# Cross-attention on Trainium2: values projected from tiles of 128 context rows across four batches, then sorted by key

## What is computed

```python
Q = (query @ Wq.T + bq).reshape(B, Sq, 16, 16).transpose(0, 2, 1, 3)
K = (key_value @ Wk.T + bk).reshape(B, Skv, 16, 16).transpose(0, 2, 1, 3)
V = (key_value @ Wv.T + bv).reshape(B, Skv, 16, 16).transpose(0, 2, 1, 3)
attn = softmax(einsum('bhqd,bhkd->bhqk', Q, K) / 4)
context = einsum('bhqk,bhkd->bhqd', attn, V).transpose(0, 2, 1, 3).reshape(B, Sq, 256)
y = context @ W_o.T + b_o + query
out = (y - mean(y)) / sqrt(var(y) + 1e-5) * ln_gamma + ln_beta
```

## Time and profile before

| | us |
|---|---|
| median of three runs | 213.75 (213.46 to 214.18) |
| the profiled execution | 215.56 |
| its span, first to last instruction | 213.5 |
| PE, DVE, ACT, POOL busy | 192.7, 175.5, 173.4, 152.6 |
| mean granted clock of TensorE | 0.98 of full speed |

### The profile page before, as it was taken

One profiled execution on the slowest core, in us unless ns is written; L12 is line 12 of the kernel. 1 busy time (PEld: TensorE's weight loads), 2 busy tenths in 40 slices (PEclk: granted clock), 3 DMA queues, 4 the chain that ended last, 5 costly groups with the idle time before them and its releaser, 6 DMA issues.

```text
span 213.5 us, 5610 instructions
## 1 busy us (share of the span) xinstructions
PE 192.7 (90%) x2070; PEld 173.8 (81%) x2070; DVE 175.5 (82%) x391; ACT 173.4 (81%) x313; POOL 152.6 (71%) x148
## 2 busy tenths in 40 slices
PE   7898999979999989989998999999999999896830
PEld 4897999869899978977988798879788979795730
DVE  5879985657797898989898989898988997982694
ACT  4588789979888979998999899989998998889130
POOL 9976542596557766896689678867887788979653
PEclk9999999999999999999999999999999999999695
DMA  5945521403656964795479438943793188111112
GB/s 183 350 101 138 146 51 40 163 28 95 204 108 176 240 205 97 186 242 159 86 195 249 136 83 206 244 136 80 187 250 71 53 217 236 54 49 54 49 49 98
DMA packets 32978, 30.39 MB, mean 142 GB/s; under 512 B 11306, under 2 KB 27672, under 8 KB 32952
## 3 DMA queue, kind: packets, MB, share of 16 engines
q1 hardware_dynamic: 31720, 28.78, 51.3%
q10 hardware_dynamic: 1232, 1.26, 2.0%
HBM read 11.32 MB, written 4.19 MB: 73 GB/s over the span
## 4 chain that ended last, share of the span: by engine, by line
PE 29%; POOL 28%; issue 16%; SPq 10%; ACT 6%; DMA 5%; DVE 4%; POOLq 0%; ACTq 0%; DVEq 0%
POOL p_l L1150 18%; PE ps_x L417 14%; PE ps_acc L417 6%; PE ps_s L417 6%; POOL result L1158 5%; SPq L341 4%; POOL rs_y L1171 3%; ACT p_h L786 3%; PE ps_d L417 3%; SPq L302 3%; DMA q_mix<-q_high 3%; DMA w_raw<-in_wkT 2%; DVE result L1016 2%; SPq L319 1%; DVE xT_l L861 1%
## 5 line engine op out<-in xcount | busy, mean ns | idle before, releaser
L1150 POOL TENSOR_TENSOR p_l<-p,p_h 128x512 f16<-128x512 f32 x80 | 95.2, 1195 | 43.2 <-ACT p_h L786 42.3
L967 DVE TENSOR_REDUCE maxima<-ps_d 128x4 f32<-128x308 f32 x128 | 57.3, 466 | 11.2 <-PE ps_d L417 9.4
L785 ACT ACTIVATE p<-ps_s 128x512 f32<-128x512 f32 x80 | 47.5, 594 | 11.2 <-PE ps_s L417 7.1
L786 ACT ACTIVATE p_h<-ps_s 128x512 f16<-128x512 f32 x80 | 47.3, 591 | 0.0
L417 PE MATMUL ps_s<-q_low,kblk 128*128 128x256 f32 x144 | 38.5, 287 | 2.0 <-issue 1.0
L417 PE MATMUL ps_acc<-vblk,p_h 128*128 128x34 f16 (+1 forms) x640 | 32.6, 183 | 0.9 <-POOL p_l L1150 0.9
L417 PEld LDWEIGHTS ps_acc<-vblk,p_h 128*128 128x128 f16 x640 | 28.0, 97 | 5.6 <-issue 1.6
L417 PE MATMUL ps_acc<-vblk,p_l 128*128 128x34 f16 (+1 forms) x320 | 30.5, 182 | 0.0
L417 PEld LDWEIGHTS ps_s<-q_low,kblk 128*128 128x128 f32 x144 | 27.0, 188 | 3.6 <-issue 1.4
L1016 DVE SCALAR_TENSOR_TENSOR result<-y,meanvar,rows_sb 128x256 f32<-128x256 f32 x30 | 28.6, 991 | 0.0
L417 PE MATMUL ps_s<-q_mix,kblk 128*128 128x256 f32 x96 | 26.3, 281 | 0.0
(11 more groups left out here) (110 smaller groups left out, 506.1 us busy)
## 6 DMA issues: line engine op xcount, KB each, us to landing
xT_raw<-in_xT SPq DMA_DIRECT2D x8, 512.0 KB, 3.8
x_rows<-in_x SPq DMA_DIRECT2D x16, 256.0 KB, 3.4
out_dram<-result SPq DMA_DIRECT2D x15, 256.0 KB, 2.2
q_mix<-q_lo SPq DMA_DIRECT2D x12, 256.0 KB, 4.7
kblk<-kT SPq DMA_DIRECT2D x64, 38.5 KB, 2.3
kblk<-kblk SPq DMA_DIRECT2D x6, 256.0 KB, 3.3
q_mix<-q_low SPq DMA_DIRECT2D x6, 256.0 KB, 4.4
q_mix<-q_high SPq DMA_DIRECT2D x6, 256.0 KB, 5.1
```

The source lines that it names most:

```text
L785: nc.scalar.activation(p32[:, n % P32SLOTS], ps_s[n % 2][:], ACT.Exp, scale=SCALE)
L786: nc.scalar.activation(p_h[:, n % PSLOTS], ps_s[n % 2][:], ACT.Exp, scale=SCALE).then_inc(exp16, 1)
L967: v_.tensor_reduce(maxima[:, t, h0:h0 + DMAX_HEADS], ps_d[((DMAX + 1) * (s + 1) + j) % 2][:, 0:DMAX_HEADS * SKV] .rearrange("p (h k) -> p ...
L1150: g_.tensor_tensor(p_l[:, n % PSLOTS], p32[:, n % P32SLOTS], p_h[:, n % PSLOTS], ALU.subtract).then_inc(rest16, 1)
```

## The change

Values are projected from tiles of 128 rows of a group's 308 context rows, whatever batch they belong to: three tiles (128, 128 and 52 rows), six matmuls each. Task `v` even takes tiles 0 and 1, odd takes tile 2 alone. ACT and POOL write to a new tile `vpack`, 128 partitions by head, group, tile, half, part and 17. A key of a batch now lies on any partition, so a new helper `sort_v(part)` brings the rows of each batch back to partitions 0 to 76 of `vparts`: six transfers per part, of 77, 51, 26, 77, 25 and 52 rows (`PIECES`), each row being 8 (part 0) or 24 (part 1) runs of 68 float16, 136 bytes. `load_v` is unchanged but waits for `v_sorted`, the landing of the sort, instead of `v_hi` and `v_lo`. POOL subtracts tasks 4 to 7 ahead of its first p_l.

```diff
+VTILES = -(-GK // P)
...
+def pieces():
+    out = []
+    for j in range(GROUP):
+        for t in range(VTILES):
+            a, b = max(P * t, SKV * j), min(P * (t + 1), SKV * (j + 1))
+            if a < b:
+                out.append((j, t, a - P * t, a - SKV * j, b - a))
+    return out
...
+        def value_rows(v):
+            return P if v % 2 == 0 else GK - 2 * P
+        def value_tiles(v):
+            return slice(0, 2) if v % 2 == 0 else slice(2, VTILES)
         def value_view(v, part):
             group = int(2 * v >= V_SPLIT)
-            b = 2 * v - V_PARTS[group][0]
-            return vparts[group][:, :, b:b + 2, :, part, 0:DK].rearrange("p h b f w -> p (b f) h w")
+            g = v // 2 - V_PARTS[group][0] // GROUP
+            return vpack[group][0:value_rows(v), :, g, value_tiles(v), :, part, 0:DK].rearrange("p h t f w -> p (t f) h w")
...
+            def sort_v(part):
+                b0, b1 = V_PARTS[part]
+                sp.wait_ge(cleared_parts, 2)
+                for done in (v_hi, v_lo):
+                    sp.wait_ge(done, b1 // 2)
+                by_batch = vparts_all[:, b0 * HH * VROW:b1 * HH * VROW].rearrange("p (x j e) -> p x j e", j=GROUP, e=VROW)
+                for j, t, row, key, n in PIECES:
+                    sp.dma_start(by_batch[key:key + n, :, j],
+                                 vpack[part][row:row + n, :, :, t].rearrange("p h g f v w -> p (h g) (f v w)")).then_inc(v_sorted[part], 16)
             def load_v(part):
                 b0, b1 = V_PARTS[part]
                 sp.wait_ge(cleared_v, (1, 4)[part])
-                for done in (v_hi, v_lo):
-                    sp.wait_ge(done, b1 // 2)
+                sp.wait_ge(v_sorted[part], 16 * NPIECE)
...
             sp.dma_start(xT_raw[:], xT_v[:, :, PAIR:2 * PAIR]).then_inc(ld_xT, 16)
+            sort_v(0)
             sp.wait_ge(cleared_k[1], 2)
...
                 if s == 0:
+                    sort_v(1)
                     load_v(1)
...
-                for j in range(2):
-                    at = (2 * n + j) * SKV
-                    ins = three(ps_acc[n][0:SKV, j * D:(j + 1) * D],
-                                lambda a, k: (c_h, c_l)[a][:, g % 2, k, at:at + SKV],
+                tiles = value_tiles(2 * g + n)
+                for t in range(tiles.start, tiles.stop):
+                    a0, a1 = P * t, min(P * (t + 1), GK)
+                    ins = three(ps_acc[n][0:a1 - a0, (t - tiles.start) * D:(t - tiles.start + 1) * D],
+                                lambda a, k: (c_h, c_l)[a][:, g % 2, k, a0:a1],
                                 lambda b, k: (wv_h, wv_l)[b][:, k, :])
...
-            for v in range(4, V_TASKS - 2):
+            for v in range(4, V_TASKS):
                 value_low(v)
...
-                    if s == 0 and u in (2, 3):
-                        value_low(V_TASKS - 4 + u)
```

More of the change, by code:

```diff
@@ L96, in segments @@
     return out
+def pieces():
[6 more added lines that the diff above has]
+    return out
+PIECES = pieces()
+NPIECE = len(PIECES)
 SEGMENTS = segments()
@@ L179, in cross_attention_kernel @@
         rs_y = sb("rs_y", [P, 2, QT], F32)
+        vpack_all = sb("vpack", [P, HH * GROUPS * VTILES * VROW], FP16)
+        vpack = [vpack_all[:, b0 // GROUP * HH * VTILES * VROW:b1 // GROUP * HH * VTILES * VROW]
+                 .rearrange("p (h g t f v w) -> p h g t f v w", h=HH, t=VTILES, f=HALVES, v=VP, w=VW) for b0, b1 in V_PARTS]
         early = ExitStack()
@@ L190, in cross_attention_kernel @@
         c_h, c_l = sb("c_h", [P, 2, KC, GK], F32R, early), sb("c_l", [P, 2, KC, GK], F32R, early)
-        vwhole = sb("vwhole", [SKV, 2, 2, D], F32, early)
+        vwhole = sb("vwhole", [P, 2, 2, D], F32, early)
         early.close()
@@ L227, in cross_attention_kernel @@
         ld_v = [sem(f"ld_v{n}") for n in range(2)]
+        v_sorted = [sem(f"v_sorted{n}") for n in range(2)]
         ld_x = [sem(f"ld_x{n}") for n in range(2)]
@@ L267, in cross_attention_kernel, with value_whole, value_sums @@
         V_TASKS = B // 2
+        def value_rows(v):
+            return P if v % 2 == 0 else GK - 2 * P
+        def value_tiles(v):
+            return slice(0, 2) if v % 2 == 0 else slice(2, VTILES)
         def value_view(v, part):
             group = int(2 * v >= V_SPLIT)
-            b = 2 * v - V_PARTS[group][0]
-            return vparts[group][:, :, b:b + 2, :, part, 0:DK].rearrange("p h b f w -> p (b f) h w")
+            g = v // 2 - V_PARTS[group][0] // GROUP
+            return vpack[group][0:value_rows(v), :, g, value_tiles(v), :, part, 0:DK].rearrange("p h t f w -> p (t f) h w")
+        def value_whole(v):
+            return vwhole[0:value_rows(v), v % 2, 0:value_tiles(v).stop - value_tiles(v).start]
+        def value_sums(v):
+            return ps_acc[v % 2][0:value_rows(v), 0:(value_tiles(v).stop - value_tiles(v).start) * D]
         def merged(t):
@@ L728, in key_hi @@
                                          bias=bk_sb[:, f:f + 1]).then_inc(k_hi, 1)
-            def value_part(v, part):
-                return value_view(v, part)
             def value_hi(v):
@@ L737, in value_hi @@
                     act.wait_ge(v_lo, v - 1)
[L738 to L741, removed]
+                scale = v_scale[0:value_rows(v), v // 2:v // 2 + 1]
+                nc.scalar.activation(value_whole(v).rearrange("p b d -> p (b d)"), value_sums(v), copy, scale=scale)
+                nc.scalar.activation(value_view(v, 0), value_sums(v).rearrange("p (c h w) -> p c h w", h=HH, w=DK),
+                                     copy, scale=scale).then_inc(v_hi, 1)
             def query_hi(f, slot):
@@ L1115, in _ @@
             g_.memset(kblk[:, 2:KSLOTS].bitcast(F32), 0.0).then_inc(cleared_k[1], 1)
-            denominators = vparts_all[:].rearrange("p (x v w) -> p x v w", v=VP, w=VW)
+            denominators = vpack_all[:].rearrange("p (x v w) -> p x v w", v=VP, w=VW)
             g_.memset(denominators[:, :, 0, DK:VW], 1.0).then_inc(cleared_parts, 1)
@@ L1124, in value_low @@
                 pool.wait_ge(v_hi, v + 1)
[L1125 removed]
+                g_.tensor_tensor(value_view(v, 1), value_whole(v).rearrange("p b (f h w) -> p (b f) h w", h=HH, w=DK),
                                  value_view(v, 0), ALU.subtract).then_inc(v_lo, 1)
```

## The result

| | before | changed |
|---|---|---|
| median of the runs | 214.03 us (213.46 to 215.33, 6 runs) | 227.44 us (226.57 to 228.63, 6 runs) |
| profiled execution, its span | 215.56 us, 213.5 us | 228.01 us, 226.0 us |
| mean granted TensorE clock | 0.980 | 0.942 |

The changed kernel takes 1.0612 times as long (95% interval 1.0581 to 1.0642): 13.4 us slower. Forecast were 226.3 us and a ratio of 1.059.

What follows compares the result with a forecast made beforehand. The prediction took SP's queue up to steps 3 and 4 as the bound: +11.3 us at `load_v(1)`, less 0.7 of slack, plus 2.0 for the clock, gives 213.75 + 12.6 = 226.3 us. The 8-in-10 range was 217 to 236 us.

Steps and rivals of the forecast that it cites:

- What bounds the kernel: SP's queue up to steps 3 and 4, almost without slack after `load_v(1)`; mostly compute afterwards, so shifts reach the end.
- PE, ACT, POOL count as nothing: Engine savings in projection and subtractions count nothing at the end, since SP's queue ends later; without that cover, 1 to 3 us.
- First sort, 4.5 us: `sort_v(0)` on SP: six issues of 0.75 us, ending 1.3 us late and shifting the queue behind by 1.3 us.
- 14 ns a packet: Price of one 136-byte sort packet on a DMA engine; 1008 on the busiest engine in part 1 take 14.1 us.
- rival 1: Sort costs only its issues, packets being cheap: second sort 6.0 us, kernel about 214.5 us; chance 0.07.
- Second sort, 16.1 us: `sort_v(1)` on SP, from 40.9 to 57.0 us: pieces queue on the busiest engine, then land before `load_v(1)` starts.
- rival 2: Sort pieces overlap, only the 51-row piece on 3 engines counts: sort 8.5 us, kernel 217 to 218.5 us; chance 0.10.
- SP held: Sign at `sort_v(1)`: SP issues its last piece long before `load_v(1)` begins; a gap under 8 us would prove it wrong.
- rival 3: Sort packets cost what 308-byte ones cost, or SP is held: 232 us at 20 ns, 245 at 28 ns; chance 0.10.
- Idle PE: PE idle some 12 us, before step 3's second product until about 77, waiting for the kT transfer.
- Clock, 2.0 us: After PE's idle time at step 3, the clock at 0.50 for 3 us costs 2.0 us, between nothing and 3.5.
- The sum: `load_v(1)` ends 11.3 us later, at 66.3; less 0.7 us of slack, plus 2.0 for the clock, 12.6 us total.

Runs made afterwards that it cites:

- Experiment 5: Changed kernel with `load_v(0)` issued ahead of `load_k(2, 1)`: 226.62 us, ratio 1.0545 to the kernel before.
- experiment 6: Changed kernel with `load_v(1)` issued behind the mixed load of step 2, and the overlay of `vparts` moved to `vpack`: 220.70 us, ratio 1.0243.
- experiment 3: Changed kernel without the sort, values in wrong rows, POOL clearing unused slots: 214.66 us, ratio 1.0034; repeated with the clearing first in POOL's program, 214.70 us, ratio 0.999.
- experiment 8: experiment 7 with `load_v(1)` cut in two, six segments behind step 2's mixed load, six behind step 4's `x_rows`: 225.00 us, ratio 1.047.
- experiment 4: Changed kernel plus 48 matmuls on zeros on PE before its wait for step 3's keys: 225.69 us, ratio 1.051.
- experiment 7: Changed kernel with the edits of Experiment 5 and experiment 6 together: 221.20 us, ratio 1.0276.
- experiment 9: Changed kernel with the 51-row piece of each sort issued last: 227.86 us, ratio 1.0621.
- Experiment 2: Changed kernel with each row of a sort piece as one run of the same bytes, values in wrong order: 221.76 us, ratio 1.0337.

## Why the prediction was right, step by step

- **What bounds the kernel.** Right for a change that makes SP later: its chain sets steps 3 and 4. Experiment 5 shows it from one side (5.6 us won at step 0 become 12.3 us of waiting), experiment 6 from the other (the same work in another order, 6.7 us). Not so for one that makes SP sooner: in experiment 3 the rest was as late without it.
- **PE, ACT, POOL count as nothing.** The term did no harm, its reason wasn't shown. They should have been worth 1 to 3 us without the cover. The engines did come 1 us sooner at the start and 1.8 us at the first weighing (experiments 5 and 8); with SP 5 us early in experiment 3 the end was no sooner, but there a clearing and `load_v(0)` stood in the way.
- **First sort, 4.5 us.** Mis-sized: 6.83 us of issues, and the copies behind it took 4.63 instead of 3.79 us. The third issue alone took 2.04 us. So `sort_v(1)` began at 43.19 instead of 40.9, and the first weighing came at 43.40 instead of 41.5. The profiled execution was the worst here: the same first sort took 5.9 to 6.5 us in experiments 4 to 8.
- **14 ns a packet.** Too dear: 10.6 ns. The forecast took its prices from the DMA share, which adds up how long each packet's record lasts. A record of this sort does last 14.0 ns, but an engine began the next packet before it ended. Three windows of the changed kernel, in which only the sort moved: 46 to 47 us (the first 77-row piece), 48 to 51 us (the 51-row piece), 54.8 to 55.4 us (the 25-row piece).

```profile
DMA packets 1016, 0.14 MB, mean 138 GB/s; under 512 B 1016, under 2 KB 1016, under 8 KB 1016
```

```profile
DMA packets 851, 0.12 MB, mean 39 GB/s; under 512 B 851, under 2 KB 851, under 8 KB 851
...
q1 hardware_dynamic: 851, 0.12, 24.8%
```

```profile
DMA packets 285, 0.04 MB, mean 65 GB/s; under 512 B 285, under 2 KB 285, under 8 KB 285
```

  On the 11, 3 and 5 engines that the forecast read from the earlier trace rows, these are one packet per engine every 10.8, 10.6 and 10.5 ns. At 14 ns they would need 14.2, 4.0 and 6.7 engines, and the last isn't a count of engines; experiment 9, where the 51-row piece ran alone, gives 10.6 ns too. The same overlap is why the share reads 0.25 where 3/16 is 0.19. That packets from 16 partitions crowd each other, by which the forecast set the 28 ns aside, no run shows. A short packet is still far from free: rival 1, and with it the rule of the Trainium skill ("DMA: Bandwidth & Descriptors", section on why small descriptors are slow) that transfers from SBUF to SBUF don't suffer from small packets, fell. Experiment 2, the same bytes in 24 times fewer runs, won 5.7 us.
- **Second sort, 16.1 us.** 14.58 us: 2.3 from the first issue to the first packet (45.47), 11.9 of packets (to 57.38; forecast 14.1), 0.4 to the next issue. That the pieces follow one another, against rival 2, was right: 1848 packets, the first piece's number, had begun by 47.48, and from there to 51.4 the rate is that of 3 engines. At 10.6 ns the 1008 packets of the busiest engine are only 10.7 us; the other 1.2 go to the hand-over between pieces and to the wide pieces, which moved one packet per ns in all and no more. That they queue on the same engines, by the lowest-numbered rule that the forecast cited (the Trainium skill, "DMA: Bandwidth & Descriptors", section on why a DMA increments its semaphore by 16), would give this order, but the trace names no engines, and SP, held in its issues, could give it too. So that stays open.
- **SP held.** The forecast's sign was that SP issues the last piece long before `load_v(1)` begins, with a gap of over 8 us. That failed: the last issue began at 53.38 and ended at 54.93, 2.84 us before `load_v(1)`. The time went into the issues (11.74 us for six) and not into the wait behind them. Being held, the half of rival 3 to which the forecast gave no price of its own, did happen. In the first sort it shows in the third issue's 2.04 us. What it cost the second by itself wasn't isolated.
- **Idle PE.** "Some 12 us" before step 3 read 6.4, because 4.4 us already stood before the first weighing, where I expected 1; it ended at 77.56, foreseen "about 77".
- **Clock, 2.0 us.** Right for the stretch that it was meant for: 1.75 by the medians of experiment 4, 2.0 within step 3. The stretch before it, from 42.7 to 53.0 us, the forecast didn't have.
- **The sum.** +12.1 at `load_v(1)`, and with the clock and the 0.7 us of slack 13.4, forecast 11.3 and 12.6. The difference of 0.8 us is the second sort's start, 2.3 us later than foreseen, less its 1.5 us of shorter length. The path was foreseen; that the total is so near is partly luck, since a first sort priced too low and packets priced too high nearly cancel: `load_v(1)` ended at 67.10, forecast 66.3.

## What to carry to other kernels

A transfer that rearranges data between two others on one queue costs its issues, its packets on its busiest engine, and the wait for its landing, and everything behind it on the queue pays all three; price it there, not by its bytes. Before placing it, write down when each transfer behind it is due, from a run in which the engines weren't late themselves: when the order of the loads was changed here, each loss was only passed to the next load that was due. Price a packet by how many of them pass in a microsecond on a known number of engines, not by the DMA share, in which packets that overlap on one engine are both counted. And price what the change is to save by itself, first: here the projection alone, in a run with an extra clearing, gave nothing, and a lead of about 2 us at step 2 is the most that any run showed.

## What the runs showed of the hardware that was not expected

- An issue of a transfer with many packets behind others can hold SP: 2.58 and 4.04 us for pieces that otherwise take 0.8, 3.06 us in another order, and none over 1.2 us with 24 times fewer packets. While SP was held, in 48 to 51 us, 13 of 16 engines stood still.
- A 136-byte packet lasted 14.0 ns, but an engine took one every 10.6 ns; and however many engines a piece had, 11 or 16, no more than about one packet per ns passed in all.
- In 4.4 us of idle PE (38.98 to 43.40) the clock fell, at 42.7, and was granted at 0.50 for 10.3 us, though PE was busy for 8.4 of them. It did so again for 10.2 us from 73.5:

```profile
42.70:53.00 10.30, 8.44 (x86) 8.08 (x87) 2.82 (x7) 4.48 (x8) 2.64 (x3) 0.50 0.60 136
53.00:73.50 20.50, 18.17 (x211) 17.03 (x209) 13.53 (x30) 15.57 (x27) 11.01 (x11) 1.00 0.50 124
73.50:83.70 10.20, 6.14 (x46) 6.01 (x47) 4.36 (x13) 3.12 (x7) 2.32 (x2) 0.50 0.74 170
```

  The forecast took the 3 us of the earlier trace rows as the length of such a stretch. The cost of the second one came out near the forecast nonetheless, because PE was waiting in the first 4 us of it anyway; what the first cost wasn't tried. Its length isn't fixed either: with the same first sort and 3.5 and 3.4 us of idle PE there, the stretch was 10.2 us in experiment 4 and 3.4 us in 6.
